# Two of 18 probability blocks a step transposed by TensorE instead of by DMA

## Chip, core and metric

One core of a Trainium2 chip runs the whole program. The metric is the device time of one execution in microseconds. Engines are named as in the profile: PE (TensorE), ACT (ScalarE), DVE (VectorE), POOL (GpSimd), SP (SyncE, which here only issues DMAs).

## What is computed

A two-layer transformer in fp32 over 1024 tokens of width 256: an attention across channels, a gated FFN, a causal attention with 32 query heads and 8 key/value heads of 64, and an FFN with ternary weights. Most of the time goes to the third, cut here to its core:

```python
scores = jnp.einsum('bqhd,bkhd->bhqk', xq, xk) * scale
scores = jnp.where(causal[None, None], scores, -jnp.inf)
probs = jax.nn.softmax(scores, axis=-1)
out = jnp.einsum('bhqk,bkhd->bqhd', probs, xv).reshape(Bx, Tx, N_HEAD * HEAD_DIM)
return out @ wo
```

## The kernel before

Precision is kept by splitting: a value becomes a high part and a low part (value minus high part), and a product is made of three products of the parts.

The causal attention runs in 64 steps G (8 for each key/value head; n = G % 8, r = G % 4). A step treats two heads of a query tile in part 0 (5 + r blocks of 128 keys per head) and of another query tile in part 1 (4 - r blocks per head), always 18 blocks of 128x128 in all. In a step:

- PE: `scores(G, 0)`, `scores(G, 1)` (L1399, L1413), each opened or closed by the mask matmuls of L1399; then side jobs in three slots, and `pv(G - 3)`, the product of transposed probabilities with the values (L1433, L1437, 54 matmuls).
- DVE: the reader of slot 2 of the step before, `row_max(G, 0)` (L1006), the reader of slot 0, `normalise_o(G - 3)` (L1013, L1015), `row_max(G, 1)`, the reader of slot 1.
- ACT: the reader of slot 0, `p_high(G - 1, 1)` (L665, probabilities to fp16), exp units 0 and 1 (L656), the reader of slot 1, exp units 2 and 3, the reader of slot 2, `p_high(G, 0)`.
- POOL: the rope sums of the step (L464, L467), then `p_low(G, 0)` and `p_low(G, 1)` (L478, probabilities minus their fp16).
- SP: `transpose_hi(G)` and `transpose_lo(G)` (L382, L386), one DMA transpose of 128 x 2304 fp16 each, once both parts are written.

`probs` and `p16` have two buffers, `pT_hi` and `pT_lo` three. PSUM banks 0 to 5 hold scores. Banks 6 and 7 form a ring for the side jobs and pv: the list RING names all entries in PE's order, an entry takes the other bank than the one before, and before an entry PE waits until the entry two places earlier has been read (`emptied`). The side jobs stand in the table JOBS (steps from 8 on):

```python
JOBS = {0: ("q1t0", "q1t1", "r0"), 1: ("r1", "r2", "ot2"), 2: ("r3", "r4", ""), 3: ("ot3", "r5", "r6"),
        4: ("kt0", "wo0", "r7"), 5: ("", "wo1", "kt1"), 6: ("q0t0", "wo2", "q0t1"), 7: ("ot0", "wo3", "ot1")}
```

q and k jobs (PE transposes, L1340) and ot jobs (L1448) are read by ACT (high part, L631, L629, L635) and then DVE (low part, L963, L960, L1021). r jobs (rope projections, L1154) and wo jobs (output projection, L1154) are read by DVE alone (L950 and L954; L1027). In a step PE does slot 0, pv, slot 1, slot 2. Each engine works strictly in the order written.

Of the kernel before, what the change touches and what calls it, by code (L numbers as in the profile page):

```python
# [19 lines left out]
ALU = mybir.AluOpType  # L20
# [3 lines left out]
P = 128  # L24
# [7 lines left out]
def transformer_program(nc, x_in, wq_a, wk_a, wv_a, wo_a, w_gate_up, w_down,  # L32
# [132 lines left out]
    with ExitStack() as ctx:  # L165
# [9 lines left out]
        def sem(name):  # L175
            return ctx.enter_context(nc.semaphore(name))
# [54 lines left out]

        scores_done, nmax_done, exp_done = sem("scores_done"), sem("nmax_done"), sem("exp_done")
        p_hi_done, p_lo_done = sem("p_hi_done"), sem("p_lo_done")
        pT_hi_landed = [sem(f"pT_hi_landed{b}") for b in range(3)]
        pT_lo_landed = [sem(f"pT_lo_landed{b}") for b in range(3)]
        pv_done, recip_done, norm_done = sem("pv_done"), sem("recip_done"), sem("norm_done")
# [32 lines left out]
        def blocks(G, part):  # L269
            r = G % 4  # L270
            return 4 - r if part else 5 + r

        def q_tile(G, part):
            return blocks(G, part) - 1

# [17 lines left out]
        def job(G, slot):  # L293
# [3 lines left out]
            name = (JOBS if G >= 8 else RAMP_JOBS)[G % 8][slot]  # L297
            return name if name and 0 <= owner(G, name) < NG else ""

        RING = []  # L300
        for G in range(STEPS):
            RING += [(G, job(G, 0))] if job(G, 0) else []
            RING += [(G, "pv")] if G >= PV_LAG else []
            RING += [(G, job(G, slot)) for slot in (1, 2) if job(G, slot)]
        RING += [(STEPS, "pv"), (STEPS + 1, "pv"), (STEPS + 1, "ot2"), (STEPS + 2, "pv"), (STEPS + 2, "ot3")]

        def side_bank(G, name):
# [37 lines left out]
        def _(sp):  # L345
# [33 lines left out]

            def transpose_hi(G):  # L380
                sp.wait_ge(p_hi_done, 2 * G + 2)
                sp.dma_start(pT_hi[G % 3][:], p16_hi[G % 2][:], transpose=True).then_inc(pT_hi_landed[G % 3], 16)  # L382

            def transpose_lo(G):
                sp.wait_ge(p_lo_done, 2 * G + 2)
                sp.dma_start(pT_lo[G % 3][:], p16_lo[G % 2][:], transpose=True).then_inc(pT_lo_landed[G % 3], 16)  # L386

            for G in range(STEPS):
                if G >= 3:
# [11 lines left out]
        def _(pool):  # L401
# [68 lines left out]

            def p_low(G, part):

                sl = part_cols(G, part)
                cols = slice(sl.start * P, sl.stop * P)
                pool.wait_ge(p_hi_done, 2 * G + part + 1)
                if G >= 2 and part == 0:
                    pool.wait_ge(pT_lo_landed[(G - 2) % 3], 16 * ((G - 2) // 3 + 1))
                nc.gpsimd.tensor_tensor(p16_lo[G % 2][:, cols], probs[G % 2][:, cols], p16_hi[G % 2][:, cols],  # L478
                                        ALU.subtract).then_inc(p_lo_done, 1)
# [48 lines left out]
        def _(act):  # L528
# [119 lines left out]
            def exp_unit(G, u):  # L648
                part, a = u // 2, u % 2
                w = blocks(G, part) * P  # L650
                start = part_cols(G, part).start * P + a * w
                act.wait_ge(nmax_done, 2 * G + part + 1)
                if G >= 2 and u == 0:
                    act.wait_ge(p_lo_done, 2 * (G - 2) + 2)
                src = SCORE_BANK[part][a] * BANK + score_pieces(G, part)[0]
                nc.scalar.activation(probs[G % 2][:, start:start + w], PS[:, src:src + w], ACT.Exp,  # L656
                                     bias=nmax[:, 4 * (G % 2) + u:4 * (G % 2) + u + 1]).then_inc(exp_done, 1)

            def p_high(G, part):
                sl = part_cols(G, part)  # L660
                cols = slice(sl.start * P, sl.stop * P)
                act.wait_ge(exp_done, 4 * G + 2 * part + 2)
                if G >= 2 and part == 0:
                    act.wait_ge(pT_hi_landed[(G - 2) % 3], 16 * ((G - 2) // 3 + 1))
                nc.scalar.copy(p16_hi[G % 2][:, cols], probs[G % 2][:, cols]).then_inc(p_hi_done, 1)  # L665

            split_wkq_high(0)
            for c in range(KC):
# [17 lines left out]
            for G in range(STEPS):  # L686
                g, n, p, r = of_step(G)
                side(G, 0)
                if G:
                    p_high(G - 1, 1)  # L690
                exp_unit(G, 0)
                exp_unit(G, 1)
                side(G, 1)
                exp_unit(G, 2)
                exp_unit(G, 3)
                side(G, 2)
                p_high(G, 0)
                if n == 5 and g + 2 < NG:
                    split_wkq_high(g + 2)
                if n == 0 and g + 2 < NG:  # L700
                    load_wkq(g + 2)
                if n == 4:
                    load_wo(g)
                if n == 2 and g:
                    split_wo_high(g - 1)
            p_high(STEPS - 1, 1)
            split_wo_high(NG - 1)
            oT_high(NG - 1, 2, side_bank(STEPS + 1, "ot2"))
            oT_high(NG - 1, 3, side_bank(STEPS + 2, "ot3"))
# [46 lines left out]
        def _(dve):  # L756
# [275 lines left out]
            def side(G, slot):  # L1032
# [12 lines left out]
                elif name[:1] == "v":  # L1045
                    v_low(int(name[-1]))

            for G in range(STEPS):
                side(G - 1, 2)
                row_max(G, 0)  # L1050
                side(G, 0)
                if G >= PV_LAG:
                    normalise_o(G - PV_LAG, side_bank(G, "pv"))
                row_max(G, 1)
                side(G, 1)
            side(STEPS - 1, 2)
            for G in range(STEPS, STEPS + PV_LAG):
                normalise_o(G - PV_LAG, side_bank(G, "pv"))
                if G == STEPS + 1:
                    oT_low(NG - 1, 2, side_bank(G, "ot2"))  # L1060
                if G == STEPS + 2:
                    oT_low(NG - 1, 3, side_bank(G, "ot3"))
# [87 lines left out]
        def _(pe):  # L1150
# [269 lines left out]
            def pv(G, b):  # L1420
# [3 lines left out]
                first = True  # L1424
                for pT, landed in ((pT_hi, pT_hi_landed), (pT_lo, pT_lo_landed)):
                    pe.wait_ge(landed[buf], 16 * turn)
                    for part in range(2):
                        n, c = blocks(G, part), part_cols(G, part).start
                        for a in range(2):
                            u = (2 * part + a) * (HEAD + 1)  # L1430
                            for j in range(n):
# [4 lines left out]
                                if pT is pT_hi:  # L1436
                                    nc.tensor.matmul(o[:, u:u + HEAD], p_block, v_lo[:, j, g * HEAD:(g + 1) * HEAD],  # L1437
                                                     start=False, stop=False, skip_group_check=True)
                last.then_inc(pv_done, 1)

            def o_transposes(gg, m, b):

# [19 lines left out]
            def emptied(G, name):  # L1462
# [2 lines left out]
                    pe.wait_ge(v_lo_done, int(name[-1]) + 1)  # L1465
                elif name == "pv":
                    pe.wait_ge(norm_done, G - PV_LAG + 1)
                elif name[:2] == "wo":
                    pe.wait_ge(x_added, 8 + 4 * owner(G, name) + int(name[-1]) + 1)
                elif name[:2] == "ot":  # L1470
# [6 lines left out]
            def side(G, name):  # L1477
# [9 lines left out]
                    values(int(name[-1]))  # L1487
                elif name == "pv":
                    pv(G - PV_LAG, b)
                elif name[:2] == "wo":  # L1490
                    out_project(owner(G, name), int(name[-1]), b)
                elif name[:2] == "ot":
# [6 lines left out]
            for G in range(STEPS):  # L1499
                scores(G, 0)  # L1500
                scores(G, 1)
                side(G, job(G, 0))
                if G >= PV_LAG:
                    side(G, "pv")
                side(G, job(G, 1))
                side(G, job(G, 2))
            side(STEPS, "pv")
            side(STEPS + 1, "pv")
            side(STEPS + 1, "ot2")
# [89 lines left out]
```

## Time and profile before

| | us |
|---|---|
| median of 3 runs (629.54 to 632.45) | 632.26 |
| the profiled execution | 630.89 |
| its span | 628.9 |

Busy in the span: PE 563.0 us (90%), PE's weight loads 484.8 (77%), DVE 461.7 (73%), POOL 450.0 (72%), ACT 434.7 (69%). In forty slices of the span:

```profile
PE   5999999987889999999999999999999868774896
DVE  4686757767768878878877887887888756519696
ACT  0624311268788898889879889888888897701894
POOL 3033436529989998998998999999999787724121
PEclk9999999999999999999999999999999999966799
DMA  9160004009999999999999999999999999950001
```

A digit is the busy share of a slice in tenths; PEclk is the granted TensorE clock in tenths. Slices 10 to 36, about 142 to 563 us, are the attention steps, and there PE, POOL and the DMA engines all show nines. The chain that ended last gives PE 33%, POOL 23%, DVE 13%, DMA 13% of the span. The time of a step is therefore to be read from the rows of single steps, not from the shares of the whole.

### The profile page before, as it was taken

To read this page: it belongs to the slowest core of one execution; us is meant where nothing else is said; L and a number is where in the kernel's file an instruction comes from. 1 tells how busy PE (TensorE), PEld (TensorE's weight loads), DVE (VectorE), ACT (ScalarE), POOL (GpSimd) and SP (SyncE) were. 2 spreads that over 40 slices of the span, in tenths; PEclk is the share of its full clock that TensorE was granted. 3 is DMA by queue.
4 is the path that set the end of the run, shared out by engine and by line. 5 is a ranking of instruction groups with operands and counts; after the bars stand their busy time and mean duration, and the time that the engine had idled before them with its cause. 6 is when DMAs were issued, how large, how long until landed. Compare 5 with 4: busy or idle time off the path is not lost.

```text
span 628.9 us, 16324 instructions
## 1 busy us (share of the span) xinstructions
PE 563.0 (90%) x6880; PEld 484.8 (77%) x6880; DVE 461.7 (73%) x764; ACT 434.7 (69%) x601; POOL 450.0 (72%) x373
## 2 busy tenths in 40 slices
PE   5999999987889999999999999999999868774896
PEld 4878888966678888888888888888889757663475
DVE  4686757767768878878877887887888756519696
ACT  0624311268788898889879889888888897701894
POOL 3033436529989998998998999999999787724121
PEclk9999999999999999999999999999999999966799
DMA  9160004009999999999999999999999999950001
GB/s 288 49 200 0 2 22 88 2 22 164 192 171 196 183 197 193 188 194 215 191 190 190 199 205 193 193 187 190 192 199 193 184 191 207 186 108 0 1 26 43
DMA packets 317192, 91.75 MB, mean 146 GB/s; under 512 B 305984, under 2 KB 316224, under 8 KB 317120
## 3 DMA queue, kind: packets, MB, share of 16 engines
q1 hardware_dynamic: 311680, 86.66, 79.3%
q10 hardware_dynamic: 5440, 4.06, 2.4%
q8 instruction: 54, 0.88, 0.5%
q14 instruction: 18, 0.15, 0.1%
HBM read 13.11 MB, written 1.05 MB: 23 GB/s over the span
## 4 chain that ended last, share of the span: by engine, by line
PE 33%; POOL 23%; DVE 13%; DMA 13%; SPq 6%; ACT 6%; issue 5%; POOLq 0%; ACTq 0%; DVEq 0%
POOL p_lo L478 17%; PE PS L1154 11%; DMA pT_lo<-p_lo 10%; DVE small L1006 4%; PE PS L1413 4%; SPq L382 4%; PE PS L1287 3%; POOL roped L467 3%; SPq L386 3%; DMA pT_hi<-p_hi 2%; PE PS L1264 2%; PE PS L1269 2%; PE PS L1265 2%; ACT probs L656 2%; PE PS L1433 2%
## 5 line engine op out<-in xcount | busy, mean ns | idle before, releaser
L478 POOL TENSOR_TENSOR p_lo<-probs,p_hi 128x1280 f16<-128x1280 f32 (+7 forms) x128 | 303.6, 2391 | 35.2 <-DMA pT_lo<-p_lo 20.5
L656 ACT ACTIVATE probs<-PS,small 128x640 f32<-128x640 f32 (+7 forms) x256 | 173.6, 743 | 43.2 <-DVE small L1006 40.1
L1006 DVE TENSOR_REDUCE small<-PS 128x2 f32<-128x1280 f32 (+7 forms) x128 | 172.8, 1351 | 22.7 <-PE PS L1413 22.1
L665 ACT CAST p_hi<-probs 128x1280 f16<-128x1280 f32 (+7 forms) x128 | 145.4, 1159 | 4.8 <-DMA pT_hi<-p_hi 4.7
L1433 PE MATMUL PS<-v_hi,pT_hi 128*128 128x65 f16 x1152 | 78.9, 195 | 1.6 <-DMA pT_hi<-p_hi 1.6
L1437 PE MATMUL PS<-v_lo,pT_hi 128*128 128x64 f16 x1152 | 78.9, 195 | 0.0
L1433 PEld LDWEIGHTS PS<-v_hi,pT_hi 128*128 128x128 f16 x1152 | 74.1, 99 | 3.3 <-issue 1.1
L1413 PE MATMUL PS<-k_hi,q_hi 64*128 64x512 f32 (+3 forms) x384 | 74.0, 381 | 1.2 <-ACT probs L656 1.2
L1437 PEld LDWEIGHTS PS<-v_lo,pT_hi 128*128 128x128 f16 x1152 | 72.6, 98 | 0.4
L1413 PE MATMUL PS<-k_hi,q_lo 64*128 64x512 f32 (+3 forms) x384 | 66.1, 339 | 0.0
L1413 PE MATMUL PS<-k_lo,q_hi 64*128 64x512 f32 (+3 forms) x384 | 66.0, 339 | 0.0
L1433 PE MATMUL PS<-v_hi,pT_lo 128*128 128x65 f16 x1152 | 46.5, 195 | 8.0 <-DMA pT_lo<-p_lo 7.9
L1154 PE MATMUL PS<-wkq_hi,xnT_hi 128*128 128x320 f32 x128 | 43.8, 342 | 8.5 <-DVE t_sin L954 3.0
L1433 PEld LDWEIGHTS PS<-v_hi,pT_lo 128*128 128x128 f16 x1152 | 40.0, 99 | 9.1 <-DMA pT_lo<-p_lo 9.1
L442 POOL TENSOR_TENSOR hT_lo<-h,hT_hi 128x512 fp32r<-128x512 f32 x16 | 23.6, 1476 | 32.7 <-DVE hT_hi L866 32.7
L467 POOL TENSOR_TENSOR roped<-t_cos,t_sin 128x256 f32<-128x256 f32 x64 | 47.0, 734 | 0.0
L1154 PE MATMUL PS<-wo_hi,oT_hi 128*128 128x256 f32 x128 | 39.8, 311 | 7.1 <-DVE oT_lo L1021 4.7
L1413 PEld LDWEIGHTS PS<-k_hi,q_hi 64*128 64x128 f32 x384 | 36.1, 184 | 12.8 <-ACT probs L656 2.0
L1399 PE MATMUL PS<-masked,picked 128*128 128x128 bf16 x256 | 36.2, 223 | 8.7 <-ACT probs L656 7.2
L1154 PE MATMUL PS<-wkq_lo,xnT_hi 128*128 128x320 f32 x128 | 39.6, 309 | 0.0
L1399 PEld LDWEIGHTS PS<-masked,picked 128*128 128x128 bf16 x256 | 16.6, 97 | 29.8 <-issue 15.7
L1154 PE MATMUL PS<-wkq_hi,xnT_lo 128*128 128x320 f32 x128 | 39.5, 308 | 0.0
(188 smaller groups left out, 1330.6 us busy)
## 6 DMA issues: line engine op xcount, KB each, us to landing
wgu_nat<-L_ffn_w_gate_up SPq DMA_DIRECT2D x2, 1024.0 KB, 9.6
wo_nat<-L_attn_wo ACTq DMA_DIRECT2D x8, 256.0 KB, 3.4
wkq_nat<-L_attn_wq ACTq DMA_DIRECT2D x6, 256.0 KB, 4.2
x<-L_attn_x SPq DMA_DIRECT2D x4, 256.0 KB, 3.8
wdn_nat<-L_ffn_w_down SPq DMA_DIRECT2D x1, 1024.0 KB, 11.3
wfc_nat<-L_ffn_w_fc SPq DMA_DIRECT2D x1, 1024.0 KB, 6.7
wpj_nat<-L_ffn_w_proj SPq DMA_DIRECT2D x1, 1024.0 KB, 9.7
pT_hi<-p_hi SPq DMA_TRANSPOSE x64, 5.6
```

Source lines behind the costliest of these rows:

```text
L382: sp.dma_start(pT_hi[G % 3][:], p16_hi[G % 2][:], transpose=True).then_inc(pT_hi_landed[G % 3], 16)
L442: nc.gpsimd.tensor_tensor(hT_lo[:, n, :], h32[:, n % 3, :], hT_hi[:, n, :].bitcast(F32), ALU.subtract).then_inc(h_lo_done, 1)
L467: nc.gpsimd.tensor_tensor(roped[:, t, P:3 * P], t_cos[b][:, 1:5, :].rearrange("p h d -> p (h d)"), t_sin[b][:, 1:5, :].rearrange("p h d -> ...
L478: nc.gpsimd.tensor_tensor(p16_lo[G % 2][:, cols], probs[G % 2][:, cols], p16_hi[G % 2][:, cols], ALU.subtract).then_inc(p_lo_done, 1)
L656: nc.scalar.activation(probs[G % 2][:, start:start + w], PS[:, src:src + w], ACT.Exp, bias=nmax[:, 4 * (G % 2) + u:4 * (G % 2) + u + 1]).t ...
L665: nc.scalar.copy(p16_hi[G % 2][:, cols], probs[G % 2][:, cols]).then_inc(p_hi_done, 1)
L1006: nc.vector.tensor_reduce(nmax[:, first:first + 2], both_heads(G, part), AX.X, ALU.max, negate=True).then_inc(nmax_done, 1)
L1154: last = nc.tensor.matmul(dst, lhsT, rhs, start=n == 0, stop=n == len(pairs) - 1)
L1399: ended = nc.tensor.matmul(b[:, at % BANK:at % BANK + P], picked[:], masked[:], start=start, stop=stop, skip_group_check=True)
L1413: last = nc.tensor.matmul(dst[a], q[rows_of[a], q_cols], k[rows_of[a], cols], start=m == 0 and not (part == 0 and ends), stop=m == 2 and n ...
L1433: last = nc.tensor.matmul(o[:, u:u + HEAD + 1], p_block, v_hi[:, j, g, :], start=first, stop=False, skip_group_check=True)
L1437: nc.tensor.matmul(o[:, u:u + HEAD], p_block, v_lo[:, j, g * HEAD:(g + 1) * HEAD], start=False, stop=False, skip_group_check=True)
```

## The change

The first two blocks of the 18 (`TURNED = 2`) leave the path over fp16 and DMA. PE transposes them in fp32 from `probs` into a ring bank (`turn`, last job of the step), ACT copies the bank into `pT_hi` as fp16 (`turned_high`), DVE subtracts and writes `pT_lo` (`turned_low`). `p_high` and `p_low` leave these 256 columns out in part 0, and the DMA transposes take 16 blocks. pv waits for both kinds. "turn" is one more entry of the ring in every step, emptied by `turned_low`.

```diff
+        turned, turned_hi, turned_lo = sem("turned"), sem("turned_hi"), sem("turned_lo")
+        def part_range(G, part):
+            at = part_cols(G, part)
+            return slice(max(at.start, TURNED) * P, at.stop * P)
+        TURNED = 2
         for G in range(STEPS):
             RING += [(G, job(G, 0))] if job(G, 0) else []
             RING += [(G, "pv")] if G >= PV_LAG else []
             RING += [(G, job(G, slot)) for slot in (1, 2) if job(G, slot)]
+            RING += [(G, "turn")]
...
-                sp.dma_start(pT_hi[G % 3][:], p16_hi[G % 2][:], transpose=True).then_inc(pT_hi_landed[G % 3], 16)
+                sp.dma_start(pT_hi[G % 3][:, TURNED:, :], p16_hi[G % 2][:, TURNED * P:],
+                             transpose=True).then_inc(pT_hi_landed[G % 3], 16)
...
             def p_low(G, part):
-                sl = part_cols(G, part)
-                cols = slice(sl.start * P, sl.stop * P)
+                cols = part_range(G, part)
...
                 if G >= 2 and u == 0:
                     act.wait_ge(p_lo_done, 2 * (G - 2) + 2)
+                    act.wait_ge(turned, G - 1)
...
             def p_high(G, part):
-                sl = part_cols(G, part)
-                cols = slice(sl.start * P, sl.stop * P)
+                cols = part_range(G, part)
...
+            def turned_high(G):
+                act.wait_ge(turned, G + 1)
+                nc.scalar.copy(pT_hi[G % 3][:, 0:TURNED, :],
+                               bank(side_bank(G, "turn"))[:, 0:TURNED * P].rearrange("p (b n) -> p b n", b=TURNED))\
+                  .then_inc(turned_hi, 1)
...
                 side(G, 0)
                 if G:
                     p_high(G - 1, 1)
+                    turned_high(G - 1)
                 exp_unit(G, 0)
...
+            def turned_low(G):
+                dve.wait_ge(turned_hi, G + 1)
+                nc.vector.tensor_tensor(pT_lo[G % 3][:, 0:TURNED, :],
+                                        bank(side_bank(G, "turn"))[:, 0:TURNED * P].rearrange("p (b n) -> p b n", b=TURNED),
+                                        pT_hi[G % 3][:, 0:TURNED, :], ALU.subtract).then_inc(turned_lo, 1)
...
                 row_max(G, 0)
+                if G:
+                    turned_low(G - 1)
                 side(G, 0)
...
                     pe.wait_ge(landed[buf], 16 * turn)
+                    pe.wait_ge(turned_hi if pT is pT_hi else turned_lo, G + 1)
...
+            def turn(G, b):
+                pe.wait_ge(exp_done, 4 * G + 1)
+                for k in range(TURNED):
+                    last = nc.tensor.transpose(bank(b)[:, k * P:(k + 1) * P], probs[G % 2][:, k * P:(k + 1) * P], identf[:])
+                last.then_inc(turned, 1)
...
                 elif name == "pv":
                     pe.wait_ge(norm_done, G - PV_LAG + 1)
+                elif name == "turn":
+                    pe.wait_ge(turned_lo, G + 1)
...
                 side(G, job(G, 1))
                 side(G, job(G, 2))
+                side(G, "turn")
```

After the last step ACT does `turned_high(63)` and DVE `turned_low(63)`.

## Rows read from the trace of the kernel before

**Rows 1.** Windows: busy of each engine, clock, DMA share, GB/s, from 223 to 551 us.

```profile
223.00:551.00 328.00, 304.28 (x4651) 269.06 (x4649) 251.55 (x369) 280.22 (x376) 300.69 (x194) 1.00 1.17 195
```

**Rows 2.** Timeline of SP: start, length of issue, line.

```profile
101.00 2.46 SPq L374 DMA_TRANSPOSE pjT<-tern  x1
...
145.55 2.69 SPq L386 DMA_TRANSPOSE pT_lo<-p_lo  x1
...
313.09 3.21 SPq L382 DMA_TRANSPOSE pT_hi<-p_hi  x1
316.37 3.75 SPq L386 DMA_TRANSPOSE pT_lo<-p_lo  x1
```

**Rows 3.** Timeline of PE: start, length, first mask matmuls of steps 8, 24, 32, 63.

```profile
184.36 0.27 PE L1399 MATMUL PS<-masked,picked 128*128 128x128 bf16 x2 [0.99 <-ACT probs L656]
...
287.80 0.28 PE L1399 MATMUL PS<-masked,picked 128*128 128x128 bf16 x2
...
339.66 0.28 PE L1399 MATMUL PS<-masked,picked 128*128 128x128 bf16 x2
...
536.75 0.29 PE L1399 MATMUL PS<-masked,picked 128*128 128x128 bf16 x2
```

**Rows 4.** Timeline of PE: first and last of five waits between steps 24 and 32.

```profile
292.86 0.41 PE L1154 MATMUL PS<-wkq_hi,xnT_hi 128*128 128x320 f32 x1 [0.27 <-DVE o L1015]
...
337.69 0.39 PE L1154 MATMUL PS<-wo_hi,oT_hi 128*128 128x256 f32 x1 [0.34 <-DVE oT_lo L1021]
```

**Rows 5.** Groups by form, 150 to 540 us: count, busy us, mean ns, idle before.

```profile
L478 POOL TENSOR_TENSOR p_lo<-probs,p_hi 128x2048 f16<-128x2048 f32 x15 | 61.6, 4106 | 10.7 <-ACT p_hi L665 7.2 <-DMA pT_lo<-p_lo 3.5
...
L1006 DVE TENSOR_REDUCE small<-PS 128x2 f32<-128x1792 f32 x15 | 30.2, 2016 | 1.3 <-PE PS L1413 1.3
...
L1015 DVE TENSOR_TENSOR o<-PS,small 128x256 f32<-128x256 f32 x60 | 25.5, 424 | 2.1
...
L665 ACT CAST p_hi<-probs 128x768 f16<-128x768 f32 x15 | 12.6, 838 | 0.0
...
L635 ACT CAST oT_hi<-PS 128x512 fp32r<-128x512 f32 x28 | 16.5, 589 | 2.7 <-PE PS L1448 1.8
...
L665 ACT CAST p_hi<-probs 128x512 f16<-128x512 f32 x15 | 9.4, 628 | 0.0
...
L665 ACT CAST p_hi<-probs 128x256 f16<-128x256 f32 x15 | 6.0, 402 | 0.0
```

**Rows 6.** Timeline of PE in step 32: job0 (q1t0) and pv's first matmul.

```profile
341.76 0.61 PE L1340 MATMUL PS<-identf,roped 128*128 128x128 f32 x4
342.21 0.19 PE L1433 MATMUL PS<-v_hi,pT_hi 128*128 128x65 f16 x1
```

**Rows 7.** Timeline of ACT in step 32: side(32, 0) and p_high(31, 1).

```profile
342.41 0.60 ACT L631 ACTIVATE q_hi<-PS 128x512 fp32r<-128x512 f32 x1 [0.16 <-PE PS L1340]
342.90 0.40 ACT L665 CAST p_hi<-probs 128x256 f16<-128x256 f32 x1
```

**Rows 8.** Timeline of DVE: the wo3 add of step 31, then step 32.

```profile
339.43 0.75 DVE L1027 SCALAR_TENSOR_TENSOR x<-PS,small,x 128x512 f32<-128x512 f32 x1 [0.91 <-PE PS L1154]
...
344.05 0.18 DVE L1013 RECIPROCAL small<-PS 128x4 f32<-128x4 f32 x1 [0.32 <-PE PS L1433]
...
345.74 0.68 DVE L963 SCALAR_TENSOR_TENSOR q_lo<-PS,q_hi 128x512 fp32r<-128x512 f32 x1
```

**Rows 9.** PE's waits in ramp and tail (timeline), then windows there.

```profile
173.64 0.63 PE L1340 MATMUL PS<-identf,roped 128*128 128x128 f32 x4 [2.19 <-POOL roped L467]
...
548.45 0.79 PE L1433 MATMUL PS<-v_hi,pT_lo 128*128 128x65 f16 x11 [2.81 <-DMA pT_lo<-p_lo]
...
171.00:174.00 3.00, 0.81 (x10) 0.53 (x9) 1.73 (x1) 1.53 (x2) 3.00 (x4) 1.00 0.71 135
548.00:550.00 2.00, 1.17 (x18) 1.01 (x18) 0.30 (x2) 0.00 (x0) 1.46 (x1) 0.50 1.10 244
```

More of the change, by code:

```diff
@@ L381, in transpose_hi @@
                 sp.wait_ge(p_hi_done, 2 * G + 2)
-                sp.dma_start(pT_hi[G % 3][:], p16_hi[G % 2][:], transpose=True).then_inc(pT_hi_landed[G % 3], 16)
+                sp.dma_start(pT_hi[G % 3][:, TURNED:, :], p16_hi[G % 2][:, TURNED * P:],
+                             transpose=True).then_inc(pT_hi_landed[G % 3], 16)
             def transpose_lo(G):
                 sp.wait_ge(p_lo_done, 2 * G + 2)
-                sp.dma_start(pT_lo[G % 3][:], p16_lo[G % 2][:], transpose=True).then_inc(pT_lo_landed[G % 3], 16)
+                sp.dma_start(pT_lo[G % 3][:, TURNED:, :], p16_lo[G % 2][:, TURNED * P:],
+                             transpose=True).then_inc(pT_lo_landed[G % 3], 16)
             for G in range(STEPS):
@@ L706, in _ @@
             p_high(STEPS - 1, 1)
+            turned_high(STEPS - 1)
             split_wo_high(NG - 1)
@@ L1056, in _ @@
             side(STEPS - 1, 2)
+            turned_low(STEPS - 1)
             for G in range(STEPS, STEPS + PV_LAG):
@@ L1489, in side @@
                     pv(G - PV_LAG, b)
+                elif name == "turn":
+                    turn(G, b)
                 elif name[:2] == "wo":
```

## The prediction, as put on record before the run

> **What bounds the kernel now.** I read the windows of the attention stretch first [rows 1]: in 223 to 551 us PE is busy 304.28 of 328 us, POOL 300.69, ACT 280.22, DVE 251.55, all at full clock. Three resources lie close together there, so I took each by its own view.
>
> The DMA queue on SP: its transposes follow one another without a gap from about 220 us on [rows 2]. One issue ends at 316.30 (313.09 + 3.21), the next starts at 316.37, and so through to the end of the stage. Such an issue took 2.69 us when nothing was queued (145.55) and takes 3.21 and 3.75 here. POOL, with the low halves, is 92% busy [rows 1].
>
> PE: from the first mask matmul of step 24 (287.80) to that of step 32 (339.66) are 51.86 us for 8 steps, 6.48 a step [rows 3]. All waits of PE's matmuls in it are five, from 0.27 to 0.80 us, together 2.25 us; the first and the last stand in [rows 4]. So PE has 49.6 us of unbroken work in 51.86. Its rows follow each other with no hole. PE bounds this stage as much as SP does, and an edit that only unburdens SP and POOL can't gain more than those 2.25 us in 8 steps.
>
> **The change part by part**, for one group of 8 steps (n = 0 to 7). Its terms are added to PE's own 49.6 us, because PE is the engine that has no spare time and is put behind a new wait.
>
> 1. SP transposes 16 blocks of 18. A 16-block transpose, that of the ternary weights, took 2.46 against 2.69 us for 18 [rows 2], so SP falls by about a tenth and is no longer a bound. POOL's part 0 loses 256 columns: 4.106/2048 x 256 = 0.51 us a step by its form [rows 5]. Neither is on PE's path, so I take 0. What hides them now is PE's own length.
>
> 2. ACT's p_high loses 256 columns, 0.628 - 0.402 = 0.23 us by its forms of 512 and 256, and gains turned_high, 128x256 out of PSUM. No such row exists. The nearest are p_high's 128x256 (0.402) and the PSUM cast of 128x512 (0.589) [rows 5], so 0.30 to 0.45, taken 0.38. DVE gains turned_low, 128x256 with one operand in PSUM, as L1015 has it (0.424) [rows 5], so 0.42, taken as 0.50 at most.
>
> 3. PE gains two fp32 128x128 transposes. Four of them started at 341.76 and what followed them started at 342.21 [rows 6]: 0.45 us for four, 0.22 for two, 1.8 us for 8 steps. They wait for exp_done of the step's first unit, long past by then. PE's work becomes 51.4 us. The bounds are 0.2 (that pitch) and 0.6 (the whole row of four).
> The Trainium skill, "TensorE: Matmul & The Clock Gate", Part 4: PE-mode transpose, gives about 275 ns for one in a kernel's context. By that the term would be 0.55 a step and the sum some 20 us more. The row here has that figure as one instruction's latency and 0.11 us as the pitch, and I go by the pitch.
>
> 4. The new job "turn" takes a place in the ring of two side banks, 6 and 7. `side(G, name)` waits until the entry two places earlier has been emptied. In every step but n = 5 the entries are ..., turn(G-1), job0(G), pv(G), so **pv(G) now waits for turned_low(G-1)**. That waits on DVE for turned_high(G-1), which on ACT comes after side(G, 0) and p_high(G-1, 1). In steps 0, 3, 4, 6 and 7, side(G, 0) reads what PE's job0(G) has just written, right ahead of pv. So PE must stand still for that whole round trip, however early all else is. Around step 32: job0 is at PE from 341.76, pv starts at 342.21 [rows 6], 0.16 us before the modelled end of job0. ACT's copy runs 342.41 to 343.01 and p_high(31, 1) 342.90 to 343.30 [rows 7]. turned_high then ends near 343.58 (0.38, less 0.1 of overlap), turned_low starts 0.04 later and ends at 344.04, and pv starts at 344.09: 1.88 us late. This is 1.48 us and p_high's own duration, which by form is 0.40 (256 columns), 0.63 (512) or 0.84 (768) in these steps [rows 5]. Steps 0, 4: 1.88 each; 3 and 7: 2.11 each; step 6: 2.32. Sum **10.3 us**. Queued behind this wait is all of PE, then normalise_o and row_max(G, 1) on DVE, then exp units 2 and 3 on ACT. This ACT time had cover from row_max; it loses that cover.
>
> 5. turn(G) itself waits for the entry two earlier, mostly job1(G), whose DVE reader stands behind row_max(G, 1). In step 7, wo3 ends at 339.39, DVE's add is 339.43 to 340.18 [rows 8], and turn could start at 339.66, where the next scores start now [rows 3]: 0.5 us late. The same for wo1, wo2: 1.5 us. In step 0, DVE ends q1t1's q_lo at 346.42, and its reciprocal, which waits for pv's end, starts at 344.05 [rows 8], so q_lo ends 2.4 us after pv, and PE is ready after about 1.3: 1.1. Step 1 has rope products in that place: 1.1. Steps 3 and 4: 0.3 together; 2: none. Sum **4.0 us**.
>
> 6. Steps 1 and 2 (job0 is a rope product that ACT doesn't read). Scores of these steps start late by term 5, DVE's row_max(G, 0), 2.02 us for the 14 blocks of step 2 [rows 5], must end ahead of turned_low, and pv waits for that. I put 0.5 and 1.0, **1.5 us**, bounds 0 and 3. Step 5 has no job0, its pv is not held and wo1 comes after turned_low anyway: 0.
>
> Sum for 8 steps: 49.6 + 1.8 + 10.3 + 4.0 + 1.5 = 67.2 us, 8.40 a step. From the scores of step 8 (184.36) to those of step 63 (536.75) [rows 3] are 55 steps in 352.4 us. They become 462.0: **+109.6**. In the steps ahead of these PE is idle for up to 2.19 us at a time [rows 9], which absorbs some; five of them hold a pv, and I put 1 us each where the rest lose 2.0: +5 (0 to 9). At the end PE waits for the transposes, 2.81 us at a time [rows 9], which a shorter queue takes away: -4 (-6 to 0). The five old waits of [rows 4] are already out of the 49.6. Total +110.6.
>
> The profiled execution took 630.89 us (span 628.9), 0.2% under the median, 632.26, of the runs: 630.9 + 110.6 = 741.5, forecast **741 us**.
>
> **The rivals.**
> - Only the fixed round trips count (terms 5 and 6 vanish, since DVE and ACT run ahead while PE stands): 49.6 + 1.8 + 10.3 = 61.7 in 8 steps, 7.71 a step, +72 in 55 steps, +73 with the two ends, about 704. For it: [rows 4] show how little PE waits for DVE now. Against it: the order of DVE is fixed, and its reader of job1 stands behind row_max. 13%.
> - The bookkeeping of PE in terms 4 to 6 is wrong since PE has real spare time. LDWEIGHTS is busy 269.06 of 328 us [rows 1], 18% spare or 1.17 us a step. If the round trip is absorbed by it, 8 steps lose 15.3 - 8 x (1.17 - 0.28) = 8.2 us, +56, about 688. The Trainium skill ("Trainium Kernel Development and Optimization", Best Practices) asks to judge PE by LDWEIGHTS busy share and not by matmul busy. Against it: the matmul rows start at an unbroken pitch and an in-order engine can't use spare array time across a wait. 4%.
> - The other side: the relief of SP and POOL decides and the new waits find their data ready. Step 5's, where the order gives it for free, would be the rule. This decides if p_high(G-1, 1) ends more than about 0.9 us (turned_high, turned_low, hand-overs) before pv would start. Then the period is PE's work, 51.4, plus about 0.3: 51.7 against 51.86, and with 4 us less at the end 626. Against it: in [rows 6, 7] p_high ends 1.1 us after pv's start, and the order of the program, not chance, puts it there. 4%: 3% below the 0.5% mark and 1% within it.
> - The clock. PE's granted clock fell from 1.00 to 0.50 (2.4 to 1.2 GHz) behind a wait of 2.81 us, but stayed at 1.00 through one of 2.19 us [rows 9]. The new waits are 1.9 to 2.3 us, in nearly every step. If the clock falls for a quarter of PE's time, a step grows by about 0.25 x 6.4 = 1.6 us, +88: about 830. 9%.
> - The forecast's mechanism with its full sum: 70%.
>
> **How the numbers follow.** The forecast's own bounds: term 2's hand-overs (0.30 to 0.45, and 0.42 to 0.50) on seven steps, -4 to +8 us in all; term 3 up to +20; terms 5 and 6 together from 2.5 to 8 us in 8 steps, -21 to +17; the beginning and the end 8 us either way. Together 715 to 765. The range should leave out no more than 2 in 10: it takes in the first rival down to 703, and leaves out the clock (9%), the two cases below (8%): **703 to 765**. This kernel can be told from no change by about 0.5%. Slower 0.96 (forecast, first rival, spare time, clock), same 0.01, faster 0.03.
>
> **What would show it.** Right: a new first wait of PE at pv's first matmul, released by DVE's turned_low, in seven of eight steps, about 1.9 to 2.3 us long in steps 0, 3, 4, 6 and 7; a wait of turn's transposes for DVE's wo add of about 0.5 us; step 5's pv without a wait; SP with gaps of over 2 us between its transposes; POOL and DVE under 75% busy; 8.4 us between the mask matmuls of one step and the next; ACT's exp unit 2 waiting for row_max by 1.5 us or more. Wrong: pv waits under 1 us, or SP still without gaps, or a granted clock under 1.00 ahead of the last step.

## The result, and the profile after

Median 741.96 us (740.78 to 750.02) against 632.26 before: ratio 1.178, 95% interval 1.174 to 1.182, slower by 110 us. The profiled execution of the changed kernel is the longest of its five, 750.0 us with a span of 748.0; the other four took 740.8 to 742.6 us. Its mean granted clock is 0.950, theirs 0.961 to 0.963. All rows of the changed kernel below are of this longest execution.

From the page after: busy time and share per engine, then the slices of the span (here 18.7 us each).

```profile
PE 608.0 (81%) x7008; PEld 517.7 (69%) x7008; DVE 487.9 (65%) x828; ACT 441.3 (59%) x665; POOL 419.2 (56%) x373
...
PE   6999999777778877878787878778778787886596
DVE  4876668676676566656665666576666656664887
ACT  1435014667776566656566666675766657770595
POOL 3144355488686468637754766487657636653321
PEclk9999999999999899989999999999999989999699
DMA  8310030488968677959685776667768767993001
```

The nines of PE and POOL in the attention steps have become sixes to eights, and DMA is down as well. No engine is full any more, which is how a loop of waits looks in this view. PEclk shows slices of 8 in the middle of the attention steps. In the kernel before it was at 9 until the last step.

Windows, with the columns of [rows 1]: the middle of the attention steps, and steps 24 to 31.

```profile
230.00:640.00 410.00, 327.21 (x4381) 282.58 (x4379) 258.73 (x399) 265.99 (x398) 256.82 (x185) 0.94 0.74 128
...
332.30:403.96 71.66, 57.46 (x762) 49.91 (x760) 44.82 (x71) 45.54 (x69) 45.54 (x34) 0.93 0.75 127
```

PE is busy 80% (327.21 of 410) where it was 93%, POOL 63%, and the granted clock is 0.94 in the mean. The eight steps take 71.66 us, for 51.86 [rows 3].

The waits of PE's matmuls in the same stretch, in total, times, longest:

```profile
PE PS L1461 <- DVE pT_lo L1068: 60.2, 38, 2.1
PE PS L1473 <- DVE x L1045: 7.2, 18, 0.4
PE PS L1473 <- DVE t_sin L972: 5.0, 5, 1.0
PE PS L1473 <- DVE q_lo L981: 2.9, 5, 0.6
```

The first line did not exist before: pv's first matmul waits for DVE's turned_low, 60.2 us in 38 waits. The three further lines are turn's own waits for the reader of job1. The four lines together are 75 us of 410.

One of these waits in order of time, at step 24 (n = 0): job0 on PE, then ACT, DVE, PE. It answers to [rows 6] and [rows 7].

```profile
334.40 0.61 PE L1367 MATMUL PS<-identf,roped 128*128 128x128 f32 x4
...
335.04 0.60 ACT L641 ACTIVATE q_hi<-PS 128x512 fp32r<-128x512 f32 x1 [1.22 <-PE PS L1367]
335.54 0.40 ACT L675 CAST p_hi<-probs 128x256 f16<-128x256 f32 x1
335.83 0.38 ACT L679 CAST pT_hi<-PS 128x256 f16<-128x256 f32 x1
...
336.24 0.42 DVE L1068 TENSOR_TENSOR pT_lo<-PS,pT_hi 128x256 f16<-128x256 f32 x1 [1.06 <-ACT pT_hi L679]
...
336.72 0.20 PE L1461 MATMUL PS<-v_hi,pT_hi 128*128 128x65 f16 x1 [1.72 <-DVE pT_lo L1068]
```

ACT copies job0's output, converts the last part of p_high, then does turned_high (0.38); DVE has been done with its row maximum since 335.18 and stands 1.06 us for ACT, then turned_low takes 0.42; pv starts 1.72 us after job0's modelled end. Nothing in this chain is late by accident: each instruction starts when the one before it ends.

turn's own wait, at the end of step 23 (n = 7), answering to [rows 8], and the first mask matmul of steps 24 and 32:

```profile
331.21 0.75 DVE L1045 SCALAR_TENSOR_TENSOR x<-PS,small,x 128x512 f32<-128x512 f32 x1 [1.35 <-PE PS L1181]
...
332.02 0.44 PE L1473 MATMUL PS<-identf,probs 128*128 128x128 f32 x2 [0.41 <-DVE x L1045]
332.30 0.28 PE L1426 MATMUL PS<-masked,picked 128*128 128x128 bf16 x2
...
403.96 0.28 PE L1426 MATMUL PS<-masked,picked 128*128 128x128 bf16 x2
```

DVE adds wo3's output until 331.96 and turn starts at 332.02, 0.41 us late.

The queue of SP, in [rows 2] without a gap, is idle between its transposes, here for 1.9 us between the two. It waits for data, and between steps 24 and 32 an issue that starts after such a gap takes 1.32 to 2.01 us:

```profile
338.15 3.54 SPq L396 DMA_TRANSPOSE pT_lo<-p_lo  x1
343.59 1.32 SPq L391 DMA_TRANSPOSE pT_hi<-p_hi  x1
```

### The profile page after: what moved, and what is told of

Its sections match the earlier page's. It is cut to its first block, busy times and chain, and to the rows that moved or that the text cites. A ratio compares the mean times of both kernels' runs of the same rounds, so it can differ in the third digit from the quotient of the medians.

```text
span 748.0 us, 16836 instructions
## 1 busy us (share of the span) xinstructions
PE 608.0 (81%) x7008; PEld 517.7 (69%) x7008; DVE 487.9 (65%) x828; ACT 441.3 (59%) x665; POOL 419.2 (56%) x373
## 4 chain that ended last, share of the span: by engine, by line
PE 57%; DVE 22%; ACT 10%; issue 8%; POOL 2%; DMA 1%; ACTq 0%; DVEq 0%
PE PS L1440 12%; PE PS L1181 11%; PE PS L1461 11%; DVE small L1024 7%; PE PS L1465 5%; ACT p_hi L675 5%; DVE pT_lo L1068 3%; PE PS L1473 3%; PE PS L1314 3%; DVE x L1045 3%; PE PS L1426 2%; PE PS L1291 2%; PE PS L1296 2%; PE PS L1292 2%; PE PS L1367 2%
## 5 line engine op out<-in xcount | busy, mean ns | idle before, releaser
L488 POOL TENSOR_TENSOR p_lo<-probs,p_hi 128x1024 f16<-128x1024 f32 (+6 forms) x128 | 271.3, 2136 | 121.3 <-ACT p_hi L675 121.3
L1461 PE MATMUL PS<-v_hi,pT_hi 128*128 128x65 f16 x1152 | 83.8, 199 | 78.9 <-DVE pT_lo L1068 77.9
L675 ACT CAST p_hi<-probs 128x1024 f16<-128x1024 f32 (+6 forms) x128 | 131.5, 1051 | 0.0
L475 POOL TENSOR_TENSOR roped<-t_cos,t_sin 128x128 f32<-128x128 f32 x64 | 29.7, 463 | 74.0 <-DVE t_sin L972 73.9
L1031 DVE RECIPROCAL small<-PS 128x4 f32<-128x4 f32 x64 | 11.7, 183 | 83.3 <-PE PS L1461 83.0
L1461 PE MATMUL PS<-v_hi,pT_lo 128*128 128x65 f16 x1152 | 52.1, 205 | 0.7 <-DMA pT_lo<-p_lo 0.7
L1181 PE MATMUL PS<-wo_hi,oT_hi 128*128 128x256 f32 x128 | 44.6, 349 | 3.3 <-POOL wo_lo L468 1.6
L1461 PEld LDWEIGHTS PS<-v_hi,pT_lo 128*128 128x128 f16 x1152 | 45.6, 105 | 0.8 <-DMA pT_lo<-p_lo 0.8
L1473 PE MATMUL PS<-identf,probs 128*128 128x128 f32 x128 | 27.8, 300 | 22.5 <-DVE x L1045 7.6
L1068 DVE TENSOR_TENSOR pT_lo<-PS,pT_hi 128x256 f16<-128x256 f32 x64 | 26.9, 421 | 25.2 <-ACT pT_hi L679 23.2
```

The lines of the kernel that those rows point to most:

```text
L475: nc.gpsimd.tensor_tensor(roped[:, t, 0:P].rearrange("p (h d) -> p h d", h=2), t_cos[b][:, 0:1, :].broadcast_to(both), t_sin[b][:, 0:1, :] ...
L1068: nc.vector.tensor_tensor(pT_lo[G % 3][:, 0:TURNED, :], bank(side_bank(G, "turn"))[:, 0:TURNED * P].rearrange("p (b n) -> p b n", b=TURNED ...
L1181: last = nc.tensor.matmul(dst, lhsT, rhs, start=n == 0, stop=n == len(pairs) - 1)
L1461: last = nc.tensor.matmul(o[:, u:u + HEAD + 1], p_block, v_hi[:, j, g, :], start=first, stop=False, skip_group_check=True)
L1473: last = nc.tensor.transpose(bank(b)[:, k * P:(k + 1) * P], probs[G % 2][:, k * P:(k + 1) * P], identf[:])
```

## Experiments

All times are medians beside runs of the kernel before on the same chip (629.6 us for the first four kernels, 631.8 for the others). "A group" is eight steps, n = 0 to 7, taken from one trace.

**1. The readers of turn moved, nothing else.**

```diff
                 if G:
                     p_high(G - 1, 1)
-                    turned_high(G - 1)
...
                 side(G, 2)
+                turned_high(G)
                 p_high(G, 0)
...
                 side(G - 1, 2)
+                if G:
+                    turned_low(G - 1)
                 row_max(G, 0)
-                if G:
-                    turned_low(G - 1)
```

> The changed kernel with the two readers of turn moved: ACT's turned_high(G) stands ahead of p_high(G, 0) in its own step instead of behind p_high(G, 1) in the next, DVE's turned_low(G) ahead of row_max(G + 1, 0). Same work, same ring. Theory of the round trip (terms 4 and 6): pv's wait of 1.7 to 2.1 us goes, turn's own waits (term 5, 4 us in 8 steps) stay, the clock stays at 1.00, about 56.5 us for 8 steps and 660 us in all (650 to 675). Rival, that the added work of ACT, DVE and PE is what costs: nothing of it is removed, so over 720 us.

655.75 us, ratio 1.042 (1.039 to 1.044). PE's longest totals of waits, then the windows of one group:

```profile
PE PS L1472 <- DVE x L1044: 6.9, 17, 0.4
PE PS L1472 <- DVE t_sin L971: 5.0, 5, 1.0
...
291.61:347.90 56.29, 52.27 (x762) 45.81 (x760) 44.77 (x71) 45.41 (x68) 45.57 (x35) 1.00 0.94 161
```

The waits of pv for turned_low are gone, turn's own are there as before, the clock is 1.00 and a group takes 56.29 us, against 56.5 expected. The same instructions at another place of the two lists give back 86 of the 110 us. This settles that most of the cost is the order, and not the work; what the clock had cost went with the waits. The group is still 4.4 us longer than the one of [rows 3]: PE is busy 52.27 us in it, where it had 49.6, and turn's own waits take 2.8.

**2. The wait without the work.** One line in the kernel before:

```diff
                     pe.wait_ge(landed[buf], 16 * turn)
+                    pe.wait_ge(p_hi_done, min(2 * (G + PV_LAG), 2 * STEPS))
```

> The kernel before with one wait added: pv(G - 3) waits until ACT has done p_high(G - 1, 1), nothing else. Theory of the round trip: PE stands in steps 0, 3, 4, 6, 7 for the wait of the change less turned_high and turned_low (0.74 us), so 1.1 to 1.6 us each, 6.6 in all, and about 0.5 in steps 1, 2 and 5: 57.8 us for 8 steps, about 670 us (655 to 685). Rival, that the ring's extra job and its work on three engines is the cost: under 640 us. The clock should stay at 1.00, as the waits are all under 2 us.

685.72 us, ratio 1.088 (1.084 to 1.091), 0.7 us above the upper bound of what was expected. PE's waits, then two groups:

```profile
PE PS L1434 <- ACT p_hi L665: 45.0, 43, 1.7
PE PS L1434 <- DVE q_lo L963: 9.7, 5, 1.9
...
248.22:307.49 59.27, 49.96 (x747) 43.64 (x745) 41.69 (x63) 44.73 (x60) 49.34 (x34) 1.00 1.01 171
307.49:368.28 60.79, 51.48 (x747) 45.17 (x745) 41.67 (x63) 44.83 (x60) 49.32 (x34) 0.97 0.98 167
```

One wait of PE for ACT, with no ring entry and no added work, costs half of what the change does. The waits in steps 0, 3, 4, 6, 7 were 1.07, 1.70, 1.07, 1.94 and 1.28 us. The groups are 59.27 and 60.79 us for 57.8 expected. They differ by 1.5 us, and the longer one shows a granted clock of 0.97, 0.50 for some 3 us behind the wait of 1.94 us. I had put all waits under 2 us on the safe side of the clock; that was wrong.

**3. Relief alone.** The changed kernel without turn and its readers; the reading index is `max(c + a * n + j, TURNED)`, so that the first two blocks are not transposed and the third is read in their place.

```diff
-            RING += [(G, "turn")]
...
-                    pe.wait_ge(turned_hi if pT is pT_hi else turned_lo, G + 1)
```

> The kernel before with 16 instead of 18 blocks through p_high, p_low and the DMA transposes and nothing in their place; left out is the transposition of the first two blocks, pv reads the third block where it would read them. PE's work is as before. If PE bounds the attention steps: 51.86 us for 8 steps fall to no less than 49.6 and the tail is 4 us shorter, 610 to 630 us. If SP or POOL bounds them: one tenth less for them, 55 steps in about 320 us, 590 to 600 us.

619.92 us, ratio 0.985 (0.983 to 0.988): inside the range of the theory that PE bounds the steps. Eight steps take 51.27 us (277.30 to 328.57), for 51.86 in [rows 3]. The group of [rows 3] is one of the longer ones: over the six groups from step 8 to 56 the mean was 51.63 us (184.36 to 494.16), so the relief gives about 0.4 us in a group. By the two traces the spans differ by 11.3 us. Of these 2.9 us lie ahead of step 8 (its first mask matmul comes at 181.51 instead of 184.36), 2.2 in the six groups, 0.7 in the last seven steps, and 5.6 behind the first mask matmul of the last step (86.6 for 92.2 us).

**4. PE's work alone.** The kernel before with two transposes in front of pv:

```diff
                 o = bank(b)
+                for k in range(2):
+                    nc.tensor.transpose(o[:, k * P:(k + 1) * P], identf[:], identf[:])
                 first = True
```

> The kernel before with two fp32 transposes of the identity into pv's own bank ahead of every pv, which overwrites them; no new wait. If PE is the bound and the pitch is 0.11 us: 0.22 us in each of 64 steps, +13 us, about 645. If one transpose costs 0.275 us of PE: +35, about 667. If PE has spare time: no change, 632.

635.33 us, ratio 1.009 (1.007 to 1.012): +5.7 us, under half of the 13 expected. A group:

```profile
283.30:335.44 52.14, 51.29 (x762) 45.93 (x760) 41.62 (x63) 44.60 (x62) 49.68 (x36) 1.00 1.20 194
```

It is 0.28 us longer than the one of [rows 3], and 0.5 longer than the mean of the six, 51.63. The first of the six is longer, 53.73 us (184.23 to 237.96), and in it the granted clock fell for some 3 us. The 1.8 us of added work went mostly into the five old waits: a rope projection behind pv that had waited 0.34 us for its ring entry (at 311.50 in the kernel before) now comes later and waits 0.13 (at 314.23). Only two waits of 0.3 us are left of the five. So PE had 49.6 us of work and 2.25 us of waits that this addition could use, as it stands ahead of them.

**5. Half the dose.** `TURNED = 1`.

> The changed kernel with TURNED = 1: one block a step by TensorE, 17 by DMA. Theory of the round trip: it is there whatever the amount, only turned_high and turned_low get shorter (by about 0.24 us together) and PE has 0.11 us less a step: 2.6 us less in 8 steps, about 724 us (708 to 736). Rival, that the cost follows the amount moved: half of the 110 us, about 687.

719.39 us, ratio 1.140 (1.136 to 1.144). One block instead of two costs 88 us instead of 110, not half. PE's first wait and a group:

```profile
PE PS L1461 <- DVE pT_lo L1068: 57.9, 42, 1.9
...
257.33:322.29 64.96, 52.07 (x754) 44.46 (x753) 43.76 (x70) 45.46 (x70) 47.52 (x34) 1.00 0.85 148
```

It is 42 waits of 1.38 us in the mean, for 38 of 1.58. In this group the clock is at 1.00.

**6 and 7. Other places for turn.** In run 6 turn(G) stands between the two halves of scores(G + 1), and turned_high(G) right behind p_high(G, 0). In run 7, besides, pv goes ahead of slot 0, but not where slot 0 is an ot job.

```diff
                 scores(G, 0)
+                if G:
+                    side(G - 1, "turn")
                 scores(G, 1)
...
+                if G:
+                    turned_high(G - 1)
                 side(G, 0)
                 if G:
                     p_high(G - 1, 1)
-                    turned_high(G - 1)
```

> The changed kernel with turn(G) moved to between scores(G + 1, 0) and scores(G + 1, 1) and turned_high(G) right behind p_high(G, 0). Theory: turn's own waits (3 us in 8 steps in the run with the early readers) go, since job1's reader is long done; pv still waits for the round trip, with the second scores and job0 as cover, so by about 0.6 us a step: about 56 us for 8 steps, 656 us (640 to 670), clock at 1.00. Rival, that it is the place of turn in the ring and not the cover that counts: over 700.

672.05 us, ratio 1.065 (1.062 to 1.068): 16 us above the estimate. PE's first wait, then DVE and PE in a step with n = 2, then one group:

```profile
PE PS L1462 <- DVE pT_lo L1069: 27.0, 24, 1.1
...
318.99 2.02 DVE L1025 TENSOR_REDUCE small<-PS 128x2 f32<-128x1792 f32 x1
320.92 0.41 DVE L1069 TENSOR_TENSOR pT_lo<-PS,pT_hi 128x256 f16<-128x256 f32 x1
...
321.39 0.20 PE L1462 MATMUL PS<-v_hi,pT_hi 128*128 128x65 f16 x1 [1.12 <-DVE pT_lo L1069]
...
302.90:361.86 58.96, 54.17 (x762) 45.00 (x760) 44.34 (x71) 45.57 (x68) 45.52 (x34) 1.00 0.90 159
```

turn's own waits are gone as expected. The cover was reckoned from ACT's side only. On DVE turned_low stands behind row_max(G, 0), which takes 2.02 us for 14 blocks and 2.3 for 16 and can't start before scores(G, 0) are done. In steps with 10 or 12 blocks pv hardly waits, in those with 14 or 16 it waits 1.1 us. That is 4.5 us in a group, no more than the 0.6 us a step of the estimate, so the waits don't explain why a group takes 58.96 us and not 56. PE's busy time does: the same instructions keep PE busy for 54.17 us, where run 1 has 52.27. The two transposes and what follows them between the halves of the scores are part of it: from the start of turn to the start of the next row are 0.37 us (318.10 to 318.47), for 0.28 in the changed kernel (332.02 to 332.30). Why PE takes longer for them there is not shown.

> As the run before it in this list, and pv(G - 3) stands ahead of slot 0 (but not where slot 0 is an ot job), with the readers on ACT and DVE moved likewise. Theory: the entry behind which the round trip is waited for is now slot 0, with pv's 1.8 us as cover, so nearly no wait is left but the normalisation for slot 1 (0.2 to 0.4 us a step) and 0.6 us in steps 3 and 7: about 54 us for 8 steps, 643 us (628 to 655). Rival, that the added work of the three engines sets it: no better than the run with the early readers, 656.

675.49 us, ratio 1.071 (1.067 to 1.075): 32 us above the estimate. PE's first wait, and one of its cases, in a step with n = 7, where slot 0 is an ot job:

```profile
PE PS L1468 <- DVE pT_lo L1072: 14.5, 12, 1.3
...
302.71 0.20 PE L1468 MATMUL PS<-v_hi,pT_hi 128*128 128x65 f16 x1 [1.27 <-DVE pT_lo L1072]
```

The ot steps wait 1.27 us for turned_low and not 0.6, by the same row maximum. A group takes 59.04 us (306.30 to 365.34) for 54 expected. PE's waits in it are 4.3 us, most of them under 0.5, and PE is busy for 54.6 us: this placement too costs PE some 2 us more than that of run 1. The time agrees with the rival, that run 7 would be no better than run 1; its reason, the added work, does not, since run 1 has the same work in 56.29 us.

**8. Relief and PE's work together, without a new wait.** Runs 3 and 4 in one kernel; as in run 3 the first two blocks are not transposed and the third is read in their place.

> Relief alone and PE's work alone together: 16 blocks through p_high, p_low and the DMA transposes (the first two blocks are not transposed, pv reads the third in their place), two fp32 transposes of the identity ahead of every pv, no new wait. It is what the change would give if its waits cost nothing. If the two effects add: 619.9 + 5.7 = 626 us (622 to 630). If the relief lets PE's full 0.22 us a step through, as SP no longer covers it: 633.

626.21 us, ratio 0.993 (0.990 to 0.996). The two effects add, within the noise. This is what moving two blocks would bring with PE's work ahead of pv and ACT's and DVE's share at no cost: 0.7% by the ratio. I found no order of the lists that comes near it and transposes all blocks; the best of them is run 1.

**9. turn right behind pv.**

```diff
                 if G >= PV_LAG:
                     side(G, "pv")
+                if G:
+                    side(G - 1, "turn")
                 side(G, job(G, 1))
```

turned_high(G - 1) goes behind exp unit 1, turned_low(G - 1) behind normalise_o.

> The changed kernel with turn(G - 1) right behind pv in step G, turned_high(G - 1) behind exp unit 1 and turned_low(G - 1) behind normalise_o, ahead of row_max(G, 1). Every ring wait then falls on something long done, except slot 1 on the normalisation (0.3 us) and slot 2 on turned_low. Theory of the ring: PE's work and little else, 53.6 us for 8 steps, and the relief, 626 to 640 us. Rival: DVE is late for row_max(G, 1) by turned_low and its wait for ACT, and ACT's exp unit 2 with it, so the loop of ACT and DVE sets the step: 650 to 675 us, with waits of PE at scores or pv.

672.64 us, ratio 1.065 (1.061 to 1.069), in the range of the rival. PE's longest waits:

```profile
PE PS L1183 <- DVE o L1034: 10.2, 24, 0.5
PE PS L1475 <- DVE oT_lo L1040: 4.6, 12, 0.5
```

Slot 1 stands where it must wait for normalise_o, up to 0.48 us, turn stands behind the reader of job0, and slot 2 behind turned_low. Each is short, and there is about one in each step: in the group from 246.76 to 305.12, of 58.36 us, they are 4.3 us together, and PE is busy for 53.60. The rival had waits of PE at scores or pv, and they are not there; only its time came true. ACT's exp units do wait more for the row maxima, 67.3 us between 200 and 560 us for 31.1 in the kernel before. Whether that loop would hold a step up if PE's waits went is not shown.

**10. The clock.** The changed kernel with the early readers of run 1, but only for turn(G) with G % 8 in 2, 5, 6, so that the longest waits of pv go and the others stay.

```diff
+        EARLY = (2, 5, 6)
...
                     p_high(G - 1, 1)
-                    turned_high(G - 1)
+                    if (G - 1) % 8 not in EARLY:
+                        turned_high(G - 1)
```

> The changed kernel with the readers early, as in the run with the early readers, but only for turn(G) with G % 8 in 2, 5, 6: the pv waits of steps 3, 6 and 7 (1.94, 2.13, 1.94 us in the changed kernel's trace) go, those of steps 0, 1, 2, 4 stay. If the granted clock costs nothing of its own: 71.6 - 6.0 = 65.6 us for 8 steps, about 706 us. If the clock fell behind just these waits and comes back to 1.00: some 4 us less again, 61.5 us for 8 steps, about 680 us.

691.56 us, ratio 1.095 (1.090 to 1.100). A group, in the columns of [rows 1]:

```profile
297.81:359.64 61.83, 52.89 (x762) 45.65 (x760) 44.43 (x70) 45.34 (x69) 45.57 (x34) 1.00 0.88 147
```

The waits that were taken out are 1.94 + 2.14 + 1.93 = 6.0 us of a group. The group became 71.66 - 61.83 = 9.8 us shorter, and its clock is 1.00 for 0.93. The remaining waits of pv are as long as they were (1.71, 0.51, 0.94, 1.71), and two of 0.34 and 0.33 us at other places are new. So 3.8 us of a group or a little more had been the clock's; PE's busy time for the same instructions went from 57.46 us to 52.89. After a wait of 2.14 us PE worked at half clock for some 3 us. In the changed kernel:

```profile
315.57 0.20 PE L1461 MATMUL PS<-v_hi,pT_hi 128*128 128x65 f16 x1 [2.14 <-DVE pT_lo L1068]
...
317.00:319.00 2.00, 2.00 (x20) 2.00 (x18) 1.21 (x3) 0.01 (x1) 1.13 (x1) 0.50 0.88 164
```

The six full groups of the changed kernel show the price of one such fall. Two of them:

```profile
260.65:332.30 71.65, 57.48 (x763) 49.90 (x761) 44.83 (x71) 45.55 (x69) 45.56 (x34) 0.93 0.76 127
475.50:544.02 68.52, 54.35 (x762) 46.80 (x760) 44.80 (x71) 45.42 (x69) 45.55 (x34) 0.98 0.75 130
```

Four groups with three falls each take 71.5 to 71.7 us, one with two 70.18, and the one with a single fall 68.52: about 1.5 us each. All 15 falls of the six groups stand behind waits of 1.93 to 2.14 us, in steps 3, 6 and 7, which are the waits that this run takes out.

For the whole run the estimate of 680 us was too low, though the group came within 0.4 us. It took the gain of six groups, which were read in an execution of 750.0 us, off the median of 742. Taken off the 750.0 it gives about 690.

## Why the prediction was right, and where only its sum was

Forecast 741 us, measured 741.96. The steps in turn:

- **What bounds the kernel** (PE as much as SP): right. Run 3 takes the load off SP and POOL and a group loses 0.4 to 0.6 us.
- **Term 1**, relief taken as 0: nearly right inside the steps, and at the end it gave 5.0 us for 4 forecast (from the last step's scores to the end 87.1 for 92.2 us). Run 3 shows another 5.7 us ahead of the last step, half of it ahead of step 8, that the changed kernel doesn't have.
- **Term 2**: right. The two added operations took 0.38 and 0.42 us, as assumed. From the groups by form of the changed kernel, 230 to 640 us:

```profile
L1068 DVE TENSOR_TENSOR pT_lo<-PS,pT_hi 128x256 f16<-128x256 f32 x47 | 19.8, 421 | 17.8 <-ACT pT_hi L679 16.3
L679 ACT CAST pT_hi<-PS 128x256 f16<-128x256 f32 x47 | 17.8, 379 | 0.0
```

- **Term 3**, PE's work: the pitch was about right, 0.28 us for the pair (332.02 to 332.30) for 0.22; its effect on the whole was not what the expectation of run 4 said. Alone it costs 5.7 us and not 13, because it can use old waits. By the 275 ns of the Trainium skill ("TensorE: Matmul & The Clock Gate", Part 4: PE-mode transpose) taken as PE's time it would have been 35, an estimate. The trace has 0.297 us for one instruction, near that figure, and 0.44 for the pair.
- **Term 4**, the round trip: right in place and size. Waits of pv in steps 0, 3, 4, 6, 7: 1.72, 1.94, 1.72, 2.14, 1.93 us. They count from the modelled end of job0; the 0.16 us that pv used to start ahead of it comes on top: 10.2 us for 10.3. Step 5's pv did not wait.
- **Term 5**, turn's waits: 0.59 and 1.00 in steps 0 and 1, 0.10 and 0.13 in 3 and 4, 0.41, 0.40 and 0.41 in 5 to 7, together 3.04 us. With 0.16 for each, as above, 4.2 us for 4.0. Its parts were less exact: the forecast had 1.1 us in each of steps 0 and 1.
- **Term 6**: 0.51 and 0.95 us for 0.5 and 1.0; with the 0.16, 1.8 for 1.5.

By these a group is 49.6 + 1.8 + 10.2 + 4.2 + 1.8 = 67.6 us (67.2 forecast), and it measured 71.66. **The clock**, a rival of its own with 9% in the prediction, came true in a mild form: not a quarter of PE's time at half clock but about an eighth (mean 0.94 over 410 us). The gap of 4.1 us agrees with what run 10 gave back and with three falls of 1.5 us. The group of 71.66 us is one of the longer ones; the six together have 15 falls, some 22 us that the sum did not have. A granted clock under 1.00 ahead of the last step was one of the prediction's own signs of being wrong, and it came true. Against it stands an error the other way. The sum took all 55 steps at the mean of a group. The first mask matmuls of steps 8 and 63 are here:

```profile
190.47 0.27 PE L1426 MATMUL PS<-masked,picked 128*128 128x128 bf16 x2
...
660.89 0.28 PE L1426 MATMUL PS<-masked,picked 128*128 128x128 bf16 x2
```

470.4 us for 462.0 forecast. Of it the six groups from step 8 to 56 took 425.1 us (190.47 to 615.53) and not 403.2; the last seven steps took 45.4 and not 58.8, since the last key/value head has no rope, k and q jobs for a next one, so that PE has less work there and slot 0 is mostly empty, which frees pv of the round trip. Already in the kernel before these seven steps were shorter than the others, 42.6 us (494.16 to 536.75), and the sum gave them the full 8.40 each. The steps ahead of step 8 cost 6.1 us for 5, and the end gave 5.0 for 4.

In short, +21.9, -13.4, +1.1 and -1.0 against the sum: the profiled execution is 119.1 us longer than the one before, for 110.6 forecast, and the forecast missed it by 8.5 us (741.5 for 750.0). The median execution is 8 us shorter than the profiled one and has the higher granted clock. From 0.950 to 0.963 over 748 us are about 10 us of PE's time at full speed, an estimate from these figures, so fewer falls of the clock would explain the 8 us; no trace of such an execution is there to show it. That the forecast met the median to 1 us is luck: there the clock that it left out and the last steps that it overpaid nearly cancel. Its mechanism is shown by runs 1, 2 and 5.

Of the other signs, pv's new first wait, turn's wait of 0.41 us, step 5, the gaps of SP and the shares of POOL and DVE (63% each) came about as written. ACT's exp unit 2 waits for the row maximum by 1.5 us or more in six of the eight steps (0.74 and 0.43 in steps 0 and 5), and a step takes 8.9 us, not 8.4, by the clock.

The rivals: "only the fixed round trips" falls, since turn's waits and those of steps 1 and 2 are there. "PE's spare time absorbs it", the one that went by the busy share of LDWEIGHTS, falls with it: weight loads had 18% of spare time before, and run 2 made the kernel 56 us slower with a wait alone. In an in-order queue with this little waiting in it, the unbroken pitch of rows told more. "The relief decides" falls by the 60.2 us that pv waits: its condition, that the new waits find their data ready, did not hold. Its price was right, 626 us where run 8 measured 626.21 without the waits.

## What to carry to other kernels

When a job is added to a ring of buffers, write down for every entry which reader must be done before the entry two places on may start, and where that reader stands in its engine's list: the price is the whole round trip over those engines if the entry behind it comes right after work that the reader's engine must treat first. Place the readers of an added job in the step that makes it, ahead of the long conversions, and test with one added wait in the old kernel before writing the new job. Sum a pipelined stretch by its kinds of steps, with the last ones apart, since they have other jobs. Compare the sum with the execution that the rows come from, and not with the median alone, as the two were 8 us apart here. And look at PE's busy time when an added job moves: between the halves of the scores the same work kept PE busy for 54.2 us in a group, at the end of the step for 52.3.

## What the runs showed of the hardware

The granted clock of TensorE fell behind waits shorter than expected. The prediction had a wait of 2.19 us in [rows 9] without a fall. In run 2 it fell behind one of 1.94 us (0.50 in the window 357 to 359 us, after pv started at 355.42), and of its five waits of 1.94 or 1.95 us three have such a fall behind them. Run 5 has waits of 1.90 to 1.94 us in every group; behind one of 1.90, which ended at 218.88, the clock fell (0.50 from 220 to 223 us), and from 230 to 600 us it is 1.00. In run 4 it fell at about 185.2 us, where PE had waited 0.48 and then 0.99 us; the kernel before has waits of 0.71 and 0.99 us at the same place and no fall. In the changed kernel's six groups no wait of 1.72 us or less has a fall behind it. In some of the changed kernel's groups it fell more often than in others: the group from 475.50 to 544.02, with one fall, took 68.52 us at a mean clock of 0.98, its neighbours 71.5 at 0.93, with three falls each. The length of one wait doesn't decide alone, then; what does is left open.

An issue of a DMA transpose of 16 blocks took 1.32 to 2.01 us in the changed kernel (332 to 404 us) where SP had been idle for 1.4 us or more before it, and 3.20 to 3.54 where it began within 0.7 us of the end of the issue before.

The same two fp32 transposes of 128x128 take PE 0.28 us to the start of the next row at the end of a step (332.02 to 332.30 in the changed kernel) and 0.37 between the halves of the scores (318.10 to 318.47 in run 6).
